# Reordering one window of the edge-attention pass: queries, feed-forward products, maxima

## What is computed

```python
def _edge_attention(xn, edge_index, ef, ew, ...):
    q, k, v = (xn @ Wq + bq), (xn @ Wk + bk), (xn @ Wv + bv)     # 8 heads of 32
    ep = ef @ We + be
    scores = jnp.einsum('ehd,ehd->eh', q[dst], k[src] + ep[:, None, :]) * scale
    scores = scores * ew[:, None]
    m = jax.ops.segment_max(scores, dst, num_segments=n)
    ex = jnp.exp(scores - m[dst])
    s = jax.ops.segment_sum(ex, dst, num_segments=n)
    out = jax.ops.segment_sum((ex / s[dst])[:, :, None] * v[src], dst, num_segments=n)
...
ff = jax.nn.relu(x @ W1 + b1) @ W2 + b2     # the mixer's feed-forward, 256 -> 1024 -> 256
```

## Time and profile before

| | before |
|---|---|
| time, median of 3 runs | 3592.3 us (3589.28 to 3593.52) |
| the profiled execution's own time | 3588.76 us |
| its span | 3587.0 us |
| mean granted TensorE clock | 0.892 of full |
| busy over the span: PE, DVE, ACT, POOL | 82%, 58%, 48%, 55% |
| the edge pass's windows | about 1901 to 3142 us of the span |

### The profile page before, as it was taken

The page is one execution under the profiler, slowest core; times in us unless marked ns, Lnnn a source line. Parts: engine busy times, 40 slices in busy tenths (PEclk is TensorE's granted clock), DMA queues, the critical chain, the costliest instruction groups (busy, mean ns, idle before and its releaser), DMA issues. The chain is left out here.

```text
span 3587.0 us, 53395 instructions
## 1 busy us (share of the span) xinstructions
PE 2944.4 (82%) x13712; PEld 2216.5 (62%) x13712; DVE 2074.2 (58%) x4446; ACT 1735.2 (48%) x4098; POOL 1963.3 (55%) x1876
## 2 busy tenths in 40 slices
PE   2777768777777689959848999999999999889898
PEld 2455545555554578736436777777777777656565
DVE  6343333333333610056658989999999999843515
ACT  2444333333334222224336767777777777652423
POOL 3777777777774345402016777777777777530010
PEclk8788786878878689979869999999999999989899
DMA  6555555555552157642047888888888888610001
GB/s 162 146 149 147 143 149 146 153 148 141 148 140 63 37 187 217 199 171 78 12 151 225 230 234 235 233 230 237 235 235 235 230 241 231 201 68 0 27 0 36
DMA packets 362145, 560.74 MB, mean 156 GB/s; under 512 B 173242, under 2 KB 231571, under 8 KB 361445
## 3 DMA queue, kind: packets, MB, share of 16 engines
q0 software_dynamic: 113216, 348.74, 34.0%
q1 hardware_dynamic: 240774, 196.75, 18.5%
q10 hardware_dynamic: 7887, 12.11, 1.0%
HBM read 500.11 MB, written 58.48 MB: 156 GB/s over the span
## 5 line engine op out<-in xcount | busy, mean ns | idle before, releaser
L3060 POOL DMA_INDIRECT store<-kv_d,src_of x832 | 906.5, 1089 | 332.3 <-issue 248.2
L860 POOL DMA_INDIRECT agg_rows<-xn_d,src_of x832 | 793.0, 953 | 268.3 <-issue 243.1
L1033 PE MATMUL agg_sums<-agg_rows,agg_member 128*128 128x257 f32 x1664 | 570.4, 488 | 279.0 <-issue 140.3
L873 ACT ACTIVATE agg_rows<-agg_rows,weight_of 128x256 f32<-128x256 f32 x832 | 374.7, 500 | 614.2 <-DMA agg_rows<-xn_d,src_of 613.4
L1033 PEld LDWEIGHTS agg_sums<-agg_rows,agg_member 128*128 128x128 f32 x1664 | 367.4, 241 | 437.3 <-issue 190.2
L924 DVE TENSOR_TENSOR acc<-acc,agg_sums 128x257 f32 x416 | 176.4, 424 | 585.6 <-PE agg_sums L1033 570.8
L3107 PE MATMUL flash_sums<-store,flash_member 128*128 128x264 f32 x1664 | 427.6, 390 | 31.0 <-DVE store L3370 23.6
L3107 PEld LDWEIGHTS flash_sums<-store,flash_member 128*128 128x128 f32 x1664 | 313.4, 191 | 95.3 <-issue 44.0
L3301 DVE TENSOR_TENSOR store<-store,flash_ep 128x1024 f32<-128x1024 f32 x208 | 253.9, 1221 | 45.6 <-DMA store<-kv_d,src_of 29.8
L3114 PE MATMUL flash_sums<-acc,ident 128*128 x832 | 269.5, 406 | 1.8 <-ACT acc L3221 1.6
L3212 ACT ACTIVATE flash_member<-lane,lane_of 128x128 f32<-128x128 f32 x832 | 264.1, 395 | 0.0
(11 more groups left out here) (493 smaller groups left out, 5039.3 us busy)
## 6 DMA issues: line engine op xcount, KB each, us to landing
moe_w<-in_L_ffn_W_dram SPq DMA_DIRECT2D x64, 512.0 KB
agg_feats<-in_ef_t_dram SPq DMA_DIRECT2D x208, 128.0 KB
flash_goal<-goal_d SPq DMA_DIRECT2D x52, 512.0 KB, 5.4
agg_rows<-xn_d,src_of POOLq DMA_INDIRECT x832, 2.8
ep_d<-agg_ep SPq DMA_DIRECT2D x52, 256.0 KB
store<-kv_d,src_of POOLq DMA_INDIRECT x832, 5.1
flash_ep<-ep_d SPq DMA_DIRECT2D x416, 32.0 KB
flash_flags<-flags_d SPq DMA_DIRECT2D x416, 32.0 KB
```

What stands on the lines that cost most here:

```text
L860: pool.indirect_dma_start(rows[:, q, 0:D], None, sh.xn_d, bass.IndirectOffsetOnAxis(ap=sh.src_of[:, c:c + 1], axis=0)).then_inc(gathered[u ...
L873: act.activation(rows[:, q, 0:D], rows[:, q, 0:D], ACT.Copy, scale=sh.weight_of[:, bass.ds((UI * i + u) * SUBS + k, 1)]).then_inc(weighted, 1)
L1033: last = pe.matmul(sums[:, j % 4, 0:W], member[:, c % (2 * BI * SUBS), :], rows[:, c % NB, :], start=(c % SUBS == 0), stop=(c % SUBS == SU ...
L3060: pool.indirect_dma_start(ring[:, s, :], None, sh.kv_d, bass.IndirectOffsetOnAxis(ap=sh.src_of[:, c:c + 1], axis=0)).then_inc(gathered[p][ ...
```

## The change

It reorders the calls in `body` on three engines and adds or removes no arithmetic. On TensorE the tile numbers and `ask(s, 0)` come directly behind the transpose; the up product is cut into two halves of eight weight loads, with `ends` between them; `ask(s, 1)` and the back product come behind `carried`, and the down product behind both. On ScalarE `belong(a, 0)` and `diag` come ahead of the relu. On VectorE `mult(s, 0)` and `add(s, 1)` change places around `lower(a)`.

```diff
+                def raise_rows(half, some):
+                    for m in some:
+                        for k in range(KB):
...
                     if a is not None:
                         pe.transpose(st, scaled[:, :], sh.ident[:, :]).then_inc(st_ready, 1)
+                    if s is not None:
+                        ask_tiles = tile_numbers(pe, s)
+                        ask(s, 0, ask_tiles)
                     if ffn is not None:
...
+                        raise_rows(half, range(0, FB // 2))
-                    if s is not None:
-                        ask_tiles = tile_numbers(pe, s)
                     if a is not None:
                         pe.wait_ge(z_ready, a.at + 1)
                         pe.matmul(ends, row_head[:, :], z[:, :, :].rearrange("p a j -> p (a j)"), start=True, stop=True
                                   ).then_inc(ends_ready, 1)
-                    if s is not None:
-                        ask(s, 0, ask_tiles)
+                    if ffn is not None:
+                        raise_rows(half, range(FB // 2, FB)).then_inc(up_ready, 1)
                     if a is not None:
                         pe.wait_ge(chain_ready, a.at + 1)
...
+                    if s is not None:
+                        ask(s, 1, ask_tiles)
+                    if a is not None:
+                        pe.wait_ge(p_ready, a.at + 1)
+                        pe.wait_ge(diag_ready, a.at + 1)
...
                     if ffn is not None:
                         pe.wait_ge(hidden_ready, 2 * i + (half + 2))
...
-                    if a is not None:
-                        pe.wait_ge(p_ready, a.at + 1)
...
-                    if s is not None:
-                        ask(s, 1, ask_tiles)
@@ ScalarE
+                    if a is not None:
+                        belong(a, 0)
+                        tiles = tile_numbers(act, a)
+                        act.wait_ge(chain_ready, a.at + 1)
+                        act.activation(diag[:, :], sh.ident[0:H, 0:H], ACT.Copy, scale=fall[:, 0:1]).then_inc(diag_ready, 1)
+                        act.activation(run[:, 0:1], run[:, WS:WS + 1], ACT.Copy)
                     if ffn is not None:
...
                         last.then_inc(hidden_ready, 1)
                     if a is not None:
-                        belong(a, 0)
...
@@ VectorE
                     if s is not None:
-                        add(s, 1)
+                        mult(s, 0)
                     if a is not None:
                         lower(a)
                     if s is not None:
-                        mult(s, 0)
+                        add(s, 1)
```

More of the change, by code:

```diff
@@ L3116, in fold @@
                               start=False, stop=True).then_inc(sums_done, 1)
+                def raise_rows(half, some):
+                    for m in some:
+                        for k in range(KB):
+                            c = (half * FB + m) * P
+                            last = pe.matmul(up[:, m * P:(m + 1) * P], w1_s[:, k, c:c + P], xt_s[:, k, :],
+                                             start=(k == 0), stop=(k == KB - 1))
+                    return last
                 def body(s, a, ffn):
@@ L3146, in body @@
                                   start=False, stop=True).then_inc(carry_ready, 1)
+                    if s is not None:
[3 more added lines that the diff above has]
+                        pe.wait_ge(diag_ready, a.at + 1)
+                        pe.matmul(pt[:, 0:P], sh.ident[:, :], scaled[:, :], start=True, stop=False)
+                        pe.matmul(pt[:, 0:P], top, minus[:, :], start=False, stop=True)
+                        pe.matmul(pt[:, P:P + H], steps[:, a.side, 4 * WS:4 * WS + P], diag[:, :], start=True, stop=True
+                                  ).then_inc(back_ready, 1)
                     if ffn is not None:
```

## The result

The changed kernel takes 3630.65 us (median of 4 runs, 3628.47 to 3632.80) against 3592.53 us for the kernel before beside it: 1.0109 times as long, 95% interval 1.0095 to 1.0122. It is 38 us slower; 25 were forecast. The profiled execution's span is 3628.2 us. From the first transpose of the pass to the last it takes 1256.0 us, where the kernel before took 1216.3; what lies around the pass agrees to 2 us.

A forecast was written before the change was run, and what follows sets the result against it. A window was VectorE's own work plus three waits, 1.48 us together. The changes, 0.67 - 0.43 + 0.26 = +0.50 us a window over 50 bodies, gave +25 us and 3618; range 3606 to 3640, widened downwards to 3590.

The forecast's parts named there:

- Sign: Whole kernel: slower 0.77, same 0.13, faster 0.10.
- the first queries (0.85): TensorE's `ask(s, 0)`: first weight load 0.85 us after the transpose, from 0.59 register load plus 0.25 to the load.
- The gather wait: VectorE's wait for gathered rows ahead of the additions, 0.53 us a window, goes, all but 0.10 for the drain.
- the late down product: TensorE's down product, moved behind the back product, runs while VectorE rescales and weighs, and costs nothing.
- the clock stayed at full: Against a 7% rival: TensorE's idle gaps lower its clock in a tenth of the windows, 32 us more, 3650.
- Edit 1: TensorE's queries ahead of the up product: register load takes 0.59 us with nothing queued, queries leave the array at 2.10.
- The rival that hung on it: Register load on TensorE costs nothing, queries start at 0.07, no change, 3590; 13%.
- the faster rival: Load free and VectorE's chain alone sets `mult`: `rescale` 0.2 us earlier, -10 us, 3582; 10%.
- Edit 2: Half the up product ahead of `ends` on TensorE: VectorE waits 0.99 us ahead of `across`, before 0.32: +0.67.
- Edit 3: VectorE's `mult(s, 0)` ahead of `lower`, `add(s, 1)` behind: wait for gathered rows 0.53 less 0.10, -0.43 us a window.
- Edit 4: TensorE's `ask(s, 1)` and back product ahead of the down product: VectorE waits 0.89 us ahead of `rescale`, before 0.63: +0.26.
- ScalarE, priced at nothing: ScalarE does the same work reordered, was idle 1.55 us ahead of the exponential; relu at about 4.4, exponential at 7.9.

The follow-up runs named there:

- experiment 1: Changed kernel with TensorE loading the tile numbers ahead of the wait for the scores: 3610.4 us, 1.0050 of the kernel before.
- experiment 4: Changed kernel with the stationary operand of `ends` widened by zeros from 8 to 128 columns: 3632.6 us, 1.0105 of the kernel before.
- experiment 11: Changed kernel with ScalarE's order as before (relu, `belong`, `diag`), rerun on another chip: 3675.1 us, 1.0224 of the kernel before.
- experiment 2: Changed kernel with `ends` ahead of the whole up product, directly behind the first queries: 3598.5 us, 1.0008 of the kernel before.
- experiment 7: Changed kernel with tile numbers loaded early and the down product halved, one half ahead of the back product, one behind the second queries: 3582.7 us, 0.9966 of the kernel before.
- experiment 3: Changed kernel with the back product ahead of the second queries: 3689.1 us, 1.0266 of the kernel before.
- experiment 6: Changed kernel with VectorE's order as before (`add(s, 1)`, `lower`, `mult(s, 0)`): 3815.7 us in one run.
- experiments 9 and 10: Changed kernel with ScalarE's old order, 4487.7 us; early-load, halved-down-product version with up product one block to three, 4481.4 us; kernel before there 4492.4 us.

## Why the prediction was right

**Sign, mechanism and order of the steps.** All held; the sizes of two terms were off. The times T at which I put the first queries (0.85), the length of each group of queries (1.25), half the up product (0.89), 0.25 from `mult` to the second queries, 1.49 from back product to `rescale`, are those of the trace to 0.03 us. The gather wait is gone, the late down product costs nothing, the clock stayed at full, and no new wait came behind `rescale`.

**Edit 1.** The load costs its place, as rows 5 and 6 had it; experiment 1 measured 20 us for it. The rule of the Trainium skill, "Advanced Engine Details and Errata", section Sequencer Loop, by which the load would have run while the transpose waited in the queue, fails on the row of line 2965 above: the load starts with the transpose, and the measurement decides. The rival that hung on it fell, and the faster rival with it.

**Edit 2, the term that was too small.** Forecast +0.67, measured +0.87 (1.19 - 0.32). The step that was mis-sized is "`ends` starts at 2.10 + 0.89 = 2.99". Its load starts at 3.21 in the mean: behind the up product's stream the load of 8 columns stands 0.31 us behind the one before it, not 0.11, and with 128 columns it does start at 3.00 (experiment 4). The 0.27 from there to `across` was right. In the row that I took it from, `ends` stood alone, so the wait in a stream could not show.

**Edit 3, the other.** Forecast -0.43, measured -0.34: from 0.53 to 0.19. I put 0.10 for the drain behind `across`; it is 0.19, and was part of the 0.53 before.

**Edit 4.** Forecast +0.26, measured +0.27.

**The sum.** 0.87 - 0.34 + 0.27 = 0.80 us a window, 50 times 40 us, against 38 measured and 25 forecast. The 13 us that were missing are the two terms of edits 2 and 3, 0.20 + 0.09 a window or 14.5 us. (25 us on the median of 3592.3 are 3617.3, not 3617.5.)

**ScalarE, priced at nothing.** That holds for the change as made. My reason named the relu as what would stand in the way; the part that carries is `diag`, which the whole back product waits for. Left where it was, it would have cost another 44 us (experiment 11), and the prediction didn't see that.

## What to carry to other kernels

Lay the chain of one period out with its start times on every engine, and ask of each moved step which result it now stands ahead of: 0.6 us of register load and 0.9 us of matmuls were harmless behind a product that waited for VectorE and cost 32 us ahead of it (experiment 2). Orders on several engines are one edit: VectorE's swap costs 6 us alone and 185 us where it is left out, and ScalarE's early `diag`, left out, costs 44. Filling an engine's idle places is worth it only if what was there isn't pushed onto the next due time; the version that split a long product around the due one, with the load early, gained 0.34% (experiment 7). And an edit that removes a gap from the trace can bring its price with it: the gap's end is not the time that counts, the start of the one who waits is (experiment 4).

## What the runs showed that was not expected

- Behind loads of 128 columns that stand 0.11 us apart, the load of a stationary operand of 8 columns stood 0.31 us behind the last. VectorE started 0.27 us behind the load of the narrow product and 0.45 behind that of the same product with 128 columns, in a stream as with the array idle (experiment 4).
- With an idle time of 1.70 us in each window TensorE's clock fell to 1.2 GHz for 3.4 us in every second window, in a fixed beat (experiment 3), and with 3.0 us in each (experiment 6). With 0.71 and 0.94 us in each window it stayed at 2.4 GHz through the stretch shown (the changed kernel). But the length of one idle time doesn't settle it: the clock also fell once in experiment 1 and twice in experiment 7, where by the matmuls' records the array had not stood idle for more than 0.85 us in that window or the one ahead of it.
- On one chip all kernels took a quarter longer (4492 against 3593 us for the kernel before), with stalls of up to 32 us in the two traces of it (experiments 9 and 10) and VectorE's instructions as long as elsewhere. The cause is open.
